# Attention over four images: probabilities of five of eight groups turned by VectorE squares and DMAs, the mix in whole fp32

## The reference

```python
xg = x.reshape(B, N_GROUPS, C // N_GROUPS, H, W)
y = ((xg - mu) * jax.lax.rsqrt(var + EPS)).reshape(B, C, H, W)
y = y * gn_gamma[None, :, None, None] + gn_beta[None, :, None, None]
qkv = jnp.einsum('bchw,dc->bdhw', y, w_qkv) + b_qkv[None, :, None, None]
scores = jnp.einsum('bnc,bcm->bnm', q, k) * C ** (-0.5)
w = jax.nn.softmax(scores, axis=-1)
a = jnp.einsum('bnm,bmc->bnc', w, v)
out = jnp.einsum('bchw,dc->bdhw', a, w_out) + b_out[None, :, None, None]
return x + out
```

## Time and profile before

| | us |
|---|---|
| median of 3 timed runs | 150.47 |
| lowest, highest | 150.11, 150.55 |
| the profiled execution, its own time | 150.05 |
| span of its trace, first to last instruction | 148.3 |

### The profile page before, as it was taken

One profiled execution on the slowest core, in us unless ns is written; L12 is line 12 of the kernel. 1 busy time (PEld: TensorE's weight loads), 2 busy tenths in 40 slices (PEclk: granted clock), 3 DMA queues, 4 the chain that ended last, 5 costly groups with the idle time before them and its releaser, 6 DMA issues.

```text
span 148.3 us, 2261 instructions
## 1 busy us (share of the span) xinstructions
PE 142.5 (96%) x797; PEld 118.8 (80%) x797; DVE 115.2 (78%) x239; ACT 88.5 (60%) x163; POOL 51.3 (35%) x61
## 2 busy tenths in 40 slices
PE   7999999899999999999999999999999999999991
PEld 7877687588988888888888888888888888887880
DVE  0697799999968789999968799988778777878502
ACT  3164778996456665876455666877555566667200
POOL 6131628573331331663332331662333333333000
PEclk9999999999999999999999999999999999999999
DMA  5940000000000100020000100010001000100011
GB/s 167 288 182 0 4 0 2 0 0 0 4 2 0 71 0 0 0 75 0 0 0 22 53 2 0 0 73 0 4 0 71 0 0 0 56 22 0 0 71 71
DMA packets 2315, 4.60 MB, mean 31 GB/s; under 512 B 384, under 2 KB 384, under 8 KB 2304
## 3 DMA queue, kind: packets, MB, share of 16 engines
q1 hardware_dynamic: 2016, 4.20, 8.0%
q10 hardware_dynamic: 288, 0.27, 0.6%
HBM read 2.36 MB, written 2.10 MB: 30 GB/s over the span
## 4 chain that ended last, share of the span: by engine, by line
PE 85%; DVE 7%; DMA 3%; ACT 2%; issue 1%; SPq 0%
PE turned L624 17%; PE mixed L646 9%; PE mixed L645 9%; PE mixed L644 9%; PE scores L614 8%; PE scores L612 8%; PE scores L611 8%; PE projected L568 4%; DVE scores L445 4%; DMA ws<-in_weights_dram 3%; DVE pt_lo L457 2%; ACT probs L278 2%; PE projected L646 1%; PE projected L645 1%; PE projected L644 1%; PE projected L592 1%
## 5 line engine op out<-in xcount | busy, mean ns | idle before, releaser
L218 POOL TENSOR_SCALAR probs<-probs,inv_sum 128x1024 f32<-128x1024 f32 x32 | 36.0, 1126 | 78.6 <-DVE inv_sum L450 78.5
L287 ACT ACTIVATE pt_hi<-turned 128x512 fp32r<-128x512 f32 x64 | 34.9, 595 | 36.6 <-PE turned L624 36.4
L445 DVE TENSOR_SCALAR_CACHE_REDUCE scores<-scores,key_bias 128x1024 f32<-128x1024 f32 x31 | 40.0, 1291 | 14.8 <-PE scores L614 14.5
L457 DVE TENSOR_TENSOR pt_lo<-turned,pt_hi 128x512 fp32r<-128x512 f32 x64 | 41.1, 683 | 1.6 <-ACT pt_hi L287 1.6
L278 ACT ACTIVATE probs<-scores,neg_max 128x1024 f32<-128x1024 f32 x32 | 35.7, 1115 | 3.4 <-DVE scores L445 2.6
L624 PEld LDWEIGHTS turned<-ident,probs 128*128 128x128 f32 x256 | 29.4, 141 | 6.8 <-issue 1.8
L624 PE MATMUL turned<-ident,probs 128*128 128x128 f32 x256 | 33.7, 274 | 0.8 <-DVE pt_lo L457 0.7
L611 PE MATMUL scores<-y_hi,z_hi 128*128 128x512 f32 x62 | 24.8, 399 | 0.0
L612 PE MATMUL scores<-y_lo,z_hi 128*128 128x512 f32 x62 | 24.4, 394 | 0.0
L644 PE MATMUL mixed<-pt_hi,v_hi 128*128 128x512 f32 x56 | 23.9, 427 | 0.0
L646 PE MATMUL mixed<-pt_hi,v_lo 128*128 128x512 f32 x56 | 22.1, 394 | 0.0
(11 more groups left out here) (145 smaller groups left out, 141.9 us busy)
## 6 DMA issues: line engine op xcount, KB each, us to landing
out_dram<-result SPq DMA_DIRECT2D x8, 256.0 KB, 2.1
xs<-in_x_dram SPq DMA_DIRECT2D x2, 512.0 KB, 6.8
xs<-in_x_dram SPq DMA_DIRECT2D x3, 256.0 KB, 5.4
xs<-in_x_dram ACTq DMA_DIRECT2D x1, 256.0 KB, 3.5
ws<-in_weights_dram SPq DMA_DIRECT2D x1, 256.0 KB, 4.0
vecs<-in_vectors_dram ACTq DMA_DIRECT2D x1, 3.0 KB, 4.2
```

The costliest lines, as they stand in the source:

```text
L218: pool.tensor_scalar(probs[:, i % RING, :], probs[:, i % RING, :], inv_sum[:, i:i + 1], 1.0, ALU.mult, ALU.mult).then_inc(s_probs, 1)
L287: act.activation(pt_hi[:, g, j * 4:(j + 1) * 4, i % QB * 128:(i % QB + 1) * 128], turned[:, j, :].rearrange("p (k n) -> p k n", n=128), AC ...
L445: dve.tensor_scalar(scores[:, i % 2, :], scores[:, i % 2, :], key_bias[:, b % 2, i:i + 1], None, ALU.subtract, ALU.min, accum_out=neg_max[ ...
L457: dve.tensor_tensor(pt_lo[to], turned[:, j, :].rearrange("p (k n) -> p k n", n=128), pt_hi[to].bitcast(fp32), ALU.subtract).then_inc(s_pt_ ...
```

## The change

Groups 1 to 5 (blocks 4 to 23) are no longer turned by PE. DVE transposes all 32x32 squares of a block's probabilities in one instruction (`flip`), ordered so that for each target partition quarter the squares lie together. When the four blocks of a group are done, 16 DMAs of 32 partitions x 1024 elements (128 KB each) move the squares between the partition quarters. SP issues eight (`swap`), ACT the other eight (`swap_across`), in the last iteration of the group. Groups 0, 6 and 7 are turned by PE as before, and DVE and ACT each copy one half to SBUF, unsplit.

The mix is one fp32 matmul of 128x512 per key tile in place of three fp32r ones; probabilities and values are kept whole (`crossed`, `v`), so the tails of both are gone. A table `MIX` says how many tiles PE mixes in which iteration: a swapped group g starts in iteration 4g + 6, group 0 has one tile in each of iterations 4 to 7. The scores and the z projection keep their three fp32r matmuls.

The z projection has now a second ACT copy (`z_full`), and POOL subtracts the head from it (`z_tail`), where DVE did this from PSUM. POOL also computes the normalised input of batches 2 and 3 (`normalised_input`), which DVE did. The projections Z0, V0, V1 and Z1 of a next batch use the `turned` banks, idle in swapped groups; `mixed` has two banks. The last block of a group is in iteration i = 3 or 7, where both DMA bursts stand. SP stores group g-2 behind the swap of group g.

```diff
+    SQ = 4
+    GROUP = QB * N
+    GROUPS_OF_FOUR = BATCHES * HALVES
+    SWAPPED = range(1, 6)
+    HOME = (0, 1, 0, 1, 0, 1, 2, 0)
+    SWAP = 16 * SQ * SQ
+    MIX = {4: [(0, 1)], 5: [(0, 1)], 6: [(0, 1)], 7: [(0, 1)], 8: [(0, 2)], 9: [(0, 2)],
+           26: [(5, 2)], 27: [(5, 3)], 28: [(5, 2)], 29: [(5, 1), (6, 1)], 30: [(6, 3)], 31: [(6, 4)]}
+    for group in range(1, 5):
+        for k, tiles in enumerate((2, 3, 2, 1) if group % 2 else (1, 2, 2, 3)):
+            MIX.setdefault(4 * group + 6 + k, []).append((group, tiles))
...
+        z_full = sb("z_full", [C, HALVES, HALF])
+        v = sb("v", [128, 2, KT, C])
...
+        crossed = sb("crossed", [128, 4, GROUP])
...
-        mixed = ps("mixed", [C, HALF])
-        projected = ps("projected", [128, HALF])
+        mixed = ps("mixed", [128, 2, HALF])
...
+        def copy_of_turned(n, j):
+            return crossed[:, HOME[n // QB], :].rearrange(
+                "p (g v u c) -> p v u g c", g=SQ, v=KT, u=QB)[:, 4 * j:4 * j + 4, n % QB, :, :]
...
+            def swap(group):
+                sp.wait_ge(s_flipped, QB * group)
+                if group > 1:
+                    sp.wait_ge(s_mixed, KT * (group - 1))
+                for k in (0, 1):
+                    for g in (0, 2, 1, 3):
+                        t = g ^ k
+                        sp.dma_start(crossed[32 * t:32 * t + 32, group % 2, g * N:(g + 1) * N],
+                                     crossed[32 * g:32 * g + 32, 2 + group % 2, t * N:(t + 1) * N]
+                                     ).then_inc(s_swapped[group % 2], 16)
+            def store(group):
+                b, g = group // HALVES, group % HALVES
+                sp.wait_ge(s_result, group + 1)
+                sp.dma_start(out_v[b, :, g * HALF:(g + 1) * HALF], result[:, g, :]).then_inc(s_stored[g], 16)
+            swap(1)
+            for group in range(2, 6):
+                swap(group)
+                store(group - 2)
...
+            def z_tail(b, h):
+                half = slice(h * HALF, (h + 1) * HALF)
+                pool.wait_ge(s_z_full, HALVES * (b - 1) + h + 1)
+                pool.tensor_tensor(z_lo[:, b % 2, half], z_full[:, h, :], z_hi[:, b % 2, half].bitcast(fp32),
+                                   ALU.subtract).then_inc(s_z_lo, 1)
...
+                    if i == (0 if b == 0 else 1) and b + 1 < BATCHES:
+                        normalised_input(b + 1)
...
+                    if i in (4, 7) and b + 1 < BATCHES:
+                        z_tail(b + 1, (i - 4) // 3)
...
+                h = 0 if job == Z0 else 1
+                half = slice(h * HALF, (h + 1) * HALF)
+                act.activation(z_hi[:, b % 2, half], bank, ACT.Identity, bias=z_bias[:, :]).then_inc(s_z_hi, 1)
+                if b >= 2:
+                    act.wait_ge(s_z_lo, HALVES * (b - 2) + h + 1)
+                act.activation(z_full[:, h, :], bank, ACT.Identity, bias=z_bias[:, :]).then_inc(s_z_full, 1)
...
+            def swap_across(group):
+                act.wait_ge(s_flipped, QB * group)
+                if group > 1:
+                    act.wait_ge(s_mixed, KT * (group - 1))
+                for k in (2, 3):
+                    for g in (0, 2, 1, 3):
+                        t = g ^ k
+                        act.dma_start(crossed[32 * t:32 * t + 32, group % 2, g * N:(g + 1) * N],
+                                      crossed[32 * g:32 * g + 32, 2 + group % 2, t * N:(t + 1) * N]
+                                      ).then_inc(s_swapped[group % 2], 16)
...
+                    if not swapped(BLOCKS * b + i):
+                        turned_copy(BLOCKS * b + i)
+                    if i % QB == QB - 1 and swapped(BLOCKS * b + i):
+                        swap_across((BLOCKS * b + i) // QB)
...
-            def turned_tails(b, i):
-                g = i // QB
-                for j in range(2):
-                    dve.wait_ge(s_pt_hi, pt_count(b, i, j))
-                    to = (slice(None), g, slice(j * 4, (j + 1) * 4), slice(i % QB * 128, (i % QB + 1) * 128))
-                    dve.tensor_tensor(pt_lo[to], turned[:, j, :].rearrange("p (k n) -> p k n", n=128),
-                                      pt_hi[to].bitcast(fp32), ALU.subtract).then_inc(s_pt_lo, 1)
...
+            def flip(n):
+                group, u = n // QB, n % QB
+                dve.wait_ge(s_probs, n + 1)
+                if group > 2:
+                    dve.wait_ge(s_swapped[group % 2], swaps(group - 2))
+                dve.transpose(crossed[:, 2 + group % 2, :].rearrange("p (tv u c) -> p tv u c", u=QB, c=32)[:, :, u, :],
+                              probs[:, n % RING, :].rearrange("p (v t r) -> p t v r", t=SQ, r=32)
+                              ).then_inc(s_flipped, 1)
...
-                    turned_tails(b, i)
+                    if not swapped(BLOCKS * b + i):
+                        turned_copy(BLOCKS * b + i)
+                    if swapped(BLOCKS * b + i + 1):
+                        flip(BLOCKS * b + i + 1)
...
-                    pe.wait_ge(s_pj_lo, job_count(b, Z0))
+                    pe.wait_ge(s_z_lo, HALVES * (b - 1) + 1)
...
-                for k in range(2 * chunk, 2 * chunk + 2):
-                    v = (slice(None), b % 2, k, slice(None))
-                    pe.matmul(bank[:, :], v_hi[v], pt_hi[:, g, k, :], start=(k == 0), stop=False)
-                    pe.matmul(bank[:, :], v_hi[v], pt_lo[:, g, k, :], start=False, stop=False)
-                    mm = pe.matmul(bank[:, :], v_lo[v], pt_hi[:, g, k, :], start=False, stop=(k == KT - 1))
-                mm.then_inc(s_mixed, 1)
...
+            def mix(group, count):
+                b, g = group // HALVES, group % HALVES
+                bank = mixed[:, g, :]
...
+                        if group in SWAPPED:
+                            pe.wait_ge(s_swapped[g], swaps(group))
+                    if k % 4 == 0 and group not in SWAPPED:
+                        pe.wait_ge(s_copied[k // 4], turns(QB * group) + QB)
+                    at = crossed[:, HOME[group], :].rearrange("p (g v u c) -> p v u g c", g=SQ, v=KT, u=QB)[:, k, :, :, :]
+                    pe.matmul(bank, v[:, b % 2, k, :], at, start=(k == 0), stop=(k == KT - 1)).then_inc(s_mixed, 1)
...
+                    for group, count in MIX.get(BLOCKS * b + i, []):
+                        mix(group, count)
+            mix(GROUPS_OF_FOUR - 1, KT)
```

More of the change, by code:

```diff
@@ L167, in job_count, with swapped, turns, swaps @@
             return JOBS * (b - 1) + job + 1
-        def pt_count(b, i, j):
-            return 2 * (BLOCKS * b + i) + j + 1
+        def swapped(n):
+            return n // QB in SWAPPED
+        def turns(n):
+            return n if n < QB else n - QB * len(SWAPPED)
+        def swaps(group):
+            return SWAP * len([g for g in SWAPPED if g <= group and g % 2 == group % 2])
+        def copy_of_turned(n, j):
+            return crossed[:, HOME[n // QB], :].rearrange(
+                "p (g v u c) -> p v u g c", g=SQ, v=KT, u=QB)[:, 4 * j:4 * j + 4, n % QB, :, :]
         @block_ctx.sync
@@ L180, in _ @@
                 sp.dma_start(xs[:, b, :], x_v[b]).then_inc(s_x[b][0], 16)
[L181 to L184, removed]
+            def swap(group):
[16 more added lines that the diff above has]
+                store(group - 2)
+            for group in range(4, GROUPS_OF_FOUR):
+                store(group)
             for g in range(HALVES):
@@ L274, in exponentials @@
             def exponentials(b, i):
                 act.wait_ge(s_max, BLOCKS * b + i + 1)
-                if BLOCKS * b + i >= RING:
-                    act.wait_ge(s_turned, 2 * (BLOCKS * b + i - RING + 1))
+                freed = BLOCKS * b + i - RING
+                if freed >= 0 and swapped(freed):
+                    act.wait_ge(s_flipped, freed - QB + 1)
+                elif freed >= 0:
+                    act.wait_ge(s_turned, 2 * (turns(freed) + 1))
                 act.activation(probs[:, i % RING, :], scores[:, i % 2, :], ACT.Exp,
@@ L291, in _, with turned_copy @@
+            def turned_copy(n):
+                act.wait_ge(s_turned, 2 * turns(n) + 1)
+                if n // QB == 6:
+                    act.wait_ge(s_swapped[0], swaps(4))
+                if n // QB == 7:
+                    act.wait_ge(s_mixed, KT * 5)
+                act.activation(copy_of_turned(n, 0), turned[:, 0, :].rearrange("p (v g c) -> p v g c", v=4, g=SQ),
+                               ACT.Copy).then_inc(s_copied[0], 1)
             act.wait_ge(s_w_turned, 1)
@@ L303, in _ @@
             act.wait_ge(s_setup, 1)
-            act.activation(z_hi[:, 0, 0:FIRST], projected[:, 0:FIRST], ACT.Identity,
+            act.activation(z_hi[:, 0, 0:FIRST], mixed[:, 1, 0:FIRST], ACT.Identity,
                            bias=z_bias[:, :]).then_inc(s_z0_hi, 1)
@@ L496, in _ @@
             dve.wait_ge(s_setup, 1)
-            first_z_tail(1, projected[:, 0:FIRST], 0, FIRST)
+            first_z_tail(1, mixed[:, 1, 0:FIRST], 0, FIRST)
```

(5 more changed lines are left out.)

278 lines of the change are left out of this document (130 added, 148 removed).

## The result

The changed kernel takes 168.66 us in the median of four runs (166.72 to 169.34) against 150.33 for the kernel before: a ratio of 1.1178, 95% interval 1.1134 to 1.1223. It is 12% slower where I had forecast 148.7 us, 1.2% faster. The ratio leaves out the longest of the four runs, which was over 1.5% above the fastest. The profiled execution took 168.37, its span is 166.6.

A forecast was written before the change was run, and what follows sets the result against it. PE was taken to bound the kernel from 30 us on; -17.4 + 10.9 + 3.5 + 1.25 = -1.8 us gave 148.3 for the profiled execution, 148.7 against the median, 1.2% less. The 8-in-10 range was 145 to 156 us.

The forecast's parts named there:

- PE's prices: On PE: 0.109 us a transposition, 0.70 a mixed fp32r tile, 0.87 an fp32 one; PE alone -6.5 us.
- the sum: Transpositions -17.4, mix +10.9, z tail waits +3.5, ACT's issues +1.25: -1.8 us on the profiled 150.05.
- Place 1: POOL's z tail before a next batch's scores: PE waits 1.75 us in batch 0, 0.87 in batches 1 and 2; 3.5 together.
- Place 2: ACT's eight DMA issues before an exponential: 0.40 us each, 3.2 in one piece; costs 1.25 us in batch 1.
- The walk: Step-by-step timing of ACT's issues on the old trace's clock: first burst just hidden, then +1.25 us in batch 1.
- The assumption that an issue can run beside an activation: On ACT, an issue can begin during the activation ahead; if not, and at 0.45 an issue, 3 us more.
- Place 3: Group 1's swap by DMA: 9.4 us at 288 GB/s against 10.4 available, hidden by 1 us; not below 252 GB/s.
- A: Rival: PE is never kept waiting, all of -6.5 us shows, 144.0 us; chance 12%.
- B: Rival: swaps late at PE's first tile of groups 1, 3, 5; half rate, 144 GB/s, about 160 us; chance 18%.
- C: Rival: DVE's squares at twice the price, 2.4 us, +7, about 156 us; chance 8%.

The follow-up runs named there:

- no_dma: Changed kernel without the 80 transfers between partitions; the mix reads squares where VectorE put them: 146.31 us, ratio 0.9747 to the kernel before.
- five_issues: short_rows with three of ACT's eight issues a group left out, SP keeping its eight: 149.16 us, ratio 0.9938 to the kernel before.
- the split: Changed kernel with SP issuing 12 transfers a group, ACT four, two at a time, and POOL's z tail ahead of the normalisation: 146.87 us, ratio 0.9768.
- all_sp: Changed kernel with all 16 transfers of a group issued by SP, none by ACT: 149.21 us, ratio 0.9907 to the kernel before.
- act_only: Changed kernel with SP's eight transfers a group left out, ACT's eight kept: 159.6 us in one execution.
- short_rows: Changed kernel, both engines issuing all transfers, but 128 elements (512 B) a row, 16 KB a transfer: 159.1 us in one execution.
- half_rows_b: Changed kernel, both engines issuing all transfers, but 512 elements (2 KB) a row, 64 KB a transfer: 164.1 us in one execution.

## Why the prediction was wrong

**PE's prices held, with a saving a little too large in sum.** At the end of the changed kernel 24 records, two a tile, belong to the last four tiles of group 6 and the eight of group 7. They span 10.46 us with the last one 0.59 long, so 0.86 a tile against my 0.87. With no_dma, which has no burst and no transfer, the last result starts at 141.43 against 145.04 before: -3.6 us, where the sum had -17.4 + 10.9 + 3.5 = -3.0. Of the 3.5, place 1 took only 2.3, so PE's own part came to -5.9 and not -6.5; a wait of 1.1 us ahead of the first z projection (no_dma's second row), which the sum does not carry, is in it.

**Place 1 held**, 1.2 us too dear: in no_dma PE waits 1.3, 0.5 and 0.5 us for the z tail in iterations 6, 14 and 22.

**Place 2 failed, by one term: "I take 0.40, thus 3.2 us in one piece".** The rows behind it, loads of 128 partitions in the head, were the nearest in name only. An issue costs 0.61 with one engine issuing and 0.82 with both; a burst took 6.6 to 7.2 us and not 3.2. The walk had shown how little was left: block 9's inverse at 45.7 against PE at 45.85, "just hidden". That was right in kind: there a burst of 3.9 us still hid (five_issues), and of the 7.1 us in the changed kernel 3.2 came out as PE's idle time. I had noted the other end at 0.45, so my bound was as wrong as the value, and I had not asked what a burst of twice the length would do. Five bursts of 34.3 us in all are 18.3 more than the 16 assumed; measured are 20 more than forecast in the profiled executions (168.37 against 148.3), the clock's part within it. five_issues cuts the bursts back to nearly the assumed length, and the time is back at the predicted one.

**The assumption that an issue can run beside an activation held**: the first issue starts at 40.65, while block 8's exponential (39.90, 1.11 long) runs until 41.0.

**Place 3 came true, but not for its reason**: no mixed tile of the changed kernel waits for DMA. The transfers moved 200 to 270 GB/s, around the 252 that I had named as the border. Group 1's kept the DMA engines busy from 41.5 to 50.6 us at 229 GB/s, that is until some 10 us after the first issue. Its first tile started at 56.47, 15.8 us after the first issue where I had 10.4: the bursts on ACT had held PE back. So the margin of 1 us was never tested.

**Rivals.** A, PE never waits: not reached; no_dma and the split come nearest. B, late transfers: not in the changed kernel, as ACT's own delay gave them time. With all issues on SP one wait of 2.3 us is for transfers, but from the time of issuing them, not from half the rate that B assumed. The Trainium skill (SBUF — State Buffer, "Door 1: The DMA port swizzle") gives 32 partitions half of the ports: the trace agrees in direction, 200 to 270 GB/s against 340 for 128 partitions, not in size. C, squares at 2.4 us: no, 1.24. The Trainium skill's one element per cycle and lane (Vector Engine (DVE) Microarchitecture Reference, section 3.8) fits it: the squares take no longer than the maximum over as many elements (1.29). The rival that I did not have was the one that came: the same mechanism as place 2 at another price.

## What to carry to other kernels

In these traces a DMA issue takes its time in the stream of the engine that issues it, 0.6 us here. Where that engine is in a loop with a fraction of a microsecond of slack, price a burst as count times the issue of the same form, put twice that as its upper end, and see who stands behind it; a queue with only stores behind it (SP here) took the same burst and more with one wait of 2.3 us. Where issues must be shared, one or two at a time between the engine's steps left no wait of PE for an exponential; eight in a row made the kernel 12% slower than before, and 13% slower than with all on SP. And a step that is "just hidden" by 0.15 us has no room for an error in its price: it is the place where the forecast's error will show.

## What the runs showed of the hardware

- A DMA issue between two places in SBUF took 0.59 to 0.61 us in the median, with one engine issuing 128 KB (all_sp, act_only) and with both issuing 16 or 64 KB (short_rows, half_rows_b); 0.64 for 128 KB of 128 partitions. The loads of the head took 0.43.
- With SP and ACT starting together, ACT's second issue took 0.82 to 0.88, whatever the bytes. With 128 KB each, the issues from the fourth on took 0.74 to 1.06 on both engines in the burst listed above; the transfers of 32 partitions moved 200 to 270 GB/s, those of 128 partitions up to 340.
- An issue of ACT started 0.36 us before the activation ahead of it ended (40.65 and 41.01).
- The granted clock was 0.57 in the 4 us from 51 on, behind an idle of 3.2 us, with PE busy throughout; behind an idle of 2.17 us it once fell to 0.54 and once stayed at 1.00. Two kernels with the same issues differed by 4.9 us of span, with PE busy for 144.1 and 138.7 us at mean clocks of 0.958 and 0.989.
